# A decoder of six stages on one Trainium2 core: another hand-written order of the steps of its two attention stages, per engine

## What is computed

```python
x = ln(x + attention_with_conv_values(x))      # stage A
x = ln(x + cosine_cross(x, ctx))               # stage B
x = ln(x + gated_ternary_ffn(x))               # stage C
x = ln(x + relu_feature_attention(x))          # stage D: 16 heads of 16, 64 features, causal
x = ln(x + cross_attention(x, ctx))            # stage E: 16 heads of 16, softmax over 256 keys
x = ln(x + top2_of_8_experts(x))               # stage F
```

## Time and profile before

| | us |
|---|---|
| median of 3 runs (1478.37 to 1487.52) | 1481.47 |
| span of the profiled execution, first to last instruction | 1473.3 |
| TensorE busy | 1311.8 (89%) |
| VectorE busy | 911.7 (62%) |
| ScalarE busy | 573.1 (39%) |
| GpSimd busy | 795.9 (54%) |

### The profile page before, as it was taken

How to read it: one execution, slowest core, us unless ns; L and a number is a source line. 1 busy time by engine, 2 the same in 40 slices (tenths; PEclk the granted TensorE clock), 3 DMA queues, 4 the chain that set the end, 5 groups by cost and what they waited for, 6 DMA issues and landing times.

```text
span 1473.3 us, 23156 instructions
## 1 busy us (share of the span) xinstructions
PE 1311.8 (89%) x9073; PEld 1113.5 (76%) x9073; DVE 911.7 (62%) x1729; ACT 573.1 (39%) x1172; POOL 795.9 (54%) x761
## 2 busy tenths in 40 slices
PE   6998999999999999988899888987884699999980
PEld 6997788888888888866666666666653699999980
DVE  4656622632442262234687787777884699999966
ACT  3566311211121121124344444433342477777742
POOL 4444566666576576523232344535565347888831
PEclk9998999999999999999899999988885799999995
DMA  5101233233343233213324324235531755666605
GB/s 177 39 18 39 73 99 122 86 101 101 107 136 100 86 100 100 75 42 83 108 64 121 94 68 111 52 110 134 144 144 36 227 203 209 231 234 227 223 15 165
DMA packets 63101, 169.53 MB, mean 115 GB/s; under 512 B 11029, under 2 KB 30735, under 8 KB 55056
## 3 DMA queue, kind: packets, MB, share of 16 engines
q1 hardware_dynamic: 52432, 122.19, 27.8%
q0 software_dynamic: 10560, 45.86, 8.8%
HBM read 138.57 MB, written 33.38 MB: 117 GB/s over the span
## 4 chain that ended last, share of the span: by engine, by line
PE 71%; DVE 16%; ACT 3%; issue 3%; POOL 2%; DMA 2%; SPq 1%; ACTq 0%; POOLq 0%; DVEq 0%
PE bank L410 16%; PE bank L412 15%; PE bank L411 15%; PE bank L1297 9%; PE bank L418 4%; PE bank L1056 3%; PE bank L1137 3%; DVE topE L1809 3%; DVE shiftE L1816 3%; DVE topE L1811 1%; PE bank L1213 1%; ACT x_tok L458 1%; PE bank L1124 1%; PE bank L1192 1%; DVE x_tok L1977 1%
## 5 line engine op out<-in xcount | busy, mean ns | idle before, releaser
L1680 DVE CAST hid_hi<-bank 128x512 fp32r<-128x512 f32 x96 | 66.4, 691 | 252.1 <-ACT bank L1412 251.0
L552 POOL TENSOR_TENSOR wpiece_lo<-wraw,wpiece_hi 128x1024 fp32r<-128x1024 f32 x88 | 211.1, 2398 | 7.3
L410 PE MATMUL bank<-hid_hi,wpiece_lo 128*128 128x512 f32 x512 | 199.3, 389 | 0.0
L412 PE MATMUL bank<-hid_hi,wpiece_hi 128*128 128x512 f32 x512 | 199.2, 389 | 0.0
L411 PE MATMUL bank<-hid_lo,wpiece_hi 128*128 128x512 f32 x512 | 199.2, 389 | 0.0
L550 POOL TENSOR_SCALAR wpiece_hi<-wraw 128x1024 fp32r<-128x1024 f32 x88 | 94.1, 1069 | 154.7 <-PE bank L412 126.7
L1412 ACT ACTIVATE bank<-bank,ffn_scales 128x512 f32<-128x512 f32 x64 | 42.4, 662 | 301.5 <-PE bank L412 301.5
L1498 ACT ACTIVATE staging<-bank 128x512 f32<-128x512 f32 x128 | 70.0, 599 | 129.4 <-PE bank L1213 117.7
L412 PEld LDWEIGHTS bank<-hid_hi,wpiece_hi 128*128 128x128 f32 x512 | 96.1, 188 | 20.1
L410 PEld LDWEIGHTS bank<-hid_hi,wpiece_lo 128*128 128x128 f32 x512 | 96.1, 188 | 20.1
L411 PEld LDWEIGHTS bank<-hid_lo,wpiece_hi 128*128 128x128 f32 x512 | 96.1, 188 | 20.0
(11 more groups left out here) (342 smaller groups left out, 3696.9 us busy)
## 6 DMA issues: line engine op xcount, KB each, us to landing
wraw<-in_C_w SPq DMA_DIRECT2D x88, 512.0 KB, 3.6
w2raw<-in_F_w SPq DMA_DIRECT2D x8, 1152.0 KB, 7.2
w1raw<-in_F_w SPq DMA_DIRECT2D x8, 1028.0 KB, 7.4
split_qk<-qk_hi SPq DMA_DIRECT2D x64, 128.0 KB, 3.8
xt_lo<-split_qk SPq DMA_DIRECT2D x8, 1024.0 KB, 6.4
xt_hi<-split_qk SPq DMA_DIRECT2D x8, 1024.0 KB, 5.1
split_qk<-qk_lo SPq DMA_DIRECT2D x32, 128.0 KB
split_qk<-ctx_raw SPq DMA_DIRECT2D x32, 128.0 KB, 3.8
```

Of the source, the lines that this page charges most:

```text
L410: pe.e.matmul(o, sl, mh, start=start and i == 0, stop=False)
L412: made = pe.e.matmul(o, sh, mh, start=False, stop=stop and i == n - 1)
L552: pool.e.tensor_tensor(pair[1], raw, f(pair[0]), ALU.subtract).then_inc(done, 1)
```

## The change

`de_steps` now takes the engine, and makes one list for each. Two tables move steps: `LATER` shifts a step by rounds, `PLACE` gives it another priority; entries under "all" hold for every engine, "dve" and "pool" for one. The start of E is d + 19 for every sequence. Bank order follows PE's list; the sets of banks are as before.

```diff
-def de_steps():
+PLACE = {
+    "all": {("DPRE", 1): 0.5, ("EDR", 0, 0): 1.5, ("EFIN", 3): -1, ("EFIN", 5): 2.5, ("EPRE", 2): 1.5, ("EPRE", 3):
+            3.5, ("PAIR", 1): 0.5, ("PAIR", 2): -0.5, ("QUAD", 0): 4.5, ("QUAD", 2): -2, ("SLOTS", 0): -1, ("XT", 0):
+            0.5},
+    "dve": {("EFIN", 2): 3.5, ("EFIN", 6): 0.5, ("PAIR", 0): 0.5},
+    "pool": {("EFIN", 1): -0.5, ("EFIN", 6): -2},
+}
+LATER = {
+    "all": {("EDR", 0, 0): 1, ("EDR", 1, 0): -1, ("EFIN", 6): -1, ("EFIN", 7): 1, ("EPRE", 0): -1, ("EPRE", 1): -1,
+            ("EPRE", 3): 1, ("PAIR", 0): 1, ("QUAD", 2): -1, ("SLOTS", 0): 1, ("SLOTS", 2): -1, ("XT", 0): -1},
+}
+def de_items():
...
-        e = d + (20 if b < B - 2 else 22)
+        e = d + (19 if b < B - 2 else 19)
...
-    return in_rounds(items)
+    return items
+def de_steps(engine):
+    order = []
+    for n, (first, prio, name, args, at) in enumerate(de_items()):
+        for step, r in enumerate(range(at) if isinstance(at, int) else at):
+            q = prio if isinstance(prio, int) or isinstance(prio, float) else prio[step]
+            key = (name, args[1], step) if name in ("DDR", "EDR") else (name, step)
+            for who in ("all", engine):
+                r += LATER.get(who, {}).get(key, 0)
+                q = PLACE.get(who, {}).get(key, q)
+            order.append((first + r, q, first, n, name, step, args))
+    return [x[4:] for x in sorted(order)]
...
-AB, DE, FS, GS = ab_steps(), de_steps(), f_steps(), g_steps()
+AB, FS, GS = ab_steps(), f_steps(), g_steps()
+DE = {e: de_steps(e) for e in ("pe", "act", "dve", "pool", "sp")}
...
-            for name, step, args in DE:
+            for name, step, args in DE["pe"]:
```

More of the change, by code:

```diff
@@ L136, in g_steps @@
     return in_rounds([(b, 0, "SUM", (b,), 3) for b in range(B)])
-AB, DE, FS, GS = ab_steps(), de_steps(), f_steps(), g_steps()
+AB, FS, GS = ab_steps(), f_steps(), g_steps()
+DE = {e: de_steps(e) for e in ("pe", "act", "dve", "pool", "sp")}
 def bank_order():
-    every, low, held, upper, wide = range(8), range(6), range(6, 8), range(4, 8), range(8, 10)
+    every, low, held, upper = range(8), range(6), range(6, 8), range(4, 8)
+    wide_f, wide_s, wide_e = range(8, 10), range(8, 10), range(8, 10)
     out = []
@@ L168, in bank_order @@
         elif name == "QUAD" and step == 0:
-            out.append((("D", "f", *args), wide))
+            out.append((("D", "f", *args), wide_f))
         elif name == "QUAD" and step < 3:
-            out.append((("D", "s", *args, step - 1), wide))
+            out.append((("D", "s", *args, step - 1), wide_s))
         elif name == "QUAD":
@@ L178, in bank_order @@
         elif name == "PAIR" and step == 0:
-            out.append((("E", "s", *args), wide))
+            out.append((("E", "s", *args), wide_e))
         elif name == "PAIR" and step == 1:
@@ L640, in pool_program @@
                 pool.e.memset(v[:, :, :, DH:DH + 1], 1.0).then_inc(s_vone, 1)
-            for name, step, args in DE:
+            for name, step, args in DE["pool"]:
                 if name == "DPRE" and step == 0 and args[0] == 1:
@@ L861, in stack_heads @@
                      held.rearrange("i r (d j) s -> (i r d) (j s)", j=4), l_qk[b % 2])
-            for name, step, args in DE:
+            for name, step, args in DE["sp"]:
                 b = args[0]
@@ L1434, in finish @@
                     ln_apply(act, stage, b, resid[b % 2 if stage == "D" else 2])
-            for name, step, args in DE:
+            for name, step, args in DE["act"]:
                 if name == "CN":
@@ L1773, in finish @@
                     ln_scale(dve, stage, b)
-            for name, step, args in DE:
+            for name, step, args in DE["dve"]:
                 if name == "CN":
```

## The result

| | before | after |
|---|---|---|
| median, us | 1483.4 (1478.4 to 1487.5, 4 runs) | 1432.8 (1430.5 to 1433.7, 4 runs) |
| span of the profiled execution | 1473.3 | 1428.7 |
| mean granted clock of TensorE | 0.94 | 0.945 |

A forecast was written before the change was run, and what follows sets the result against it. TensorE was taken as nearly the bound, VectorE close behind, with waits for VectorE's shift deciding. Terms -5 - 13 - 8 = -26 gave a span of 1447.3 and, 8.2 above it, a median of 1455.5 us; range 1440 to 1476.

The forecast's parts named there:

- part 2: Attention stage: transposes and attention products one round closer to the scores; no wait added on TensorE, cost 0.
- part 1: Steady stretch: features late and D scores 1 first in the next odd round; -13 us.
- Part 1, the waits: Steady stretch: 10 of the 12.6 us that D scores wait for VectorE's shift taken as gone.
- Part 1, the clock: Steady stretch: fewer waits should leave fewer stretches at TensorE's lower clock; 3 us, ends 0 and 15.
- part 4: End of attention: sequences 6 and 7 start two rounds sooner; -8 us, ends 0 and -11.
- the 9.7 us: Steady stretch: E scores' waits for VectorE's shift, left unchanged; ends all gone or 11 us more.
- Part 3: Start of attention: keys a round sooner, context ahead of the norm; -5 us, ends -5.1 and +3.
- rival (c): End of attention: sequence 7 waits for its stack, so the end gains nothing; 1463.5 us, chance 0.10.
- Rival (a), the lock: Odd rounds: POOL's clamp blocks VectorE's through shared ports, losing 1.05 us each; slower, 1501.5 us, chance 0.07.
- Rival (b): Steady stretch: the same lock at half the time, part 1 comes to nothing; 1468.5 us, chance 0.18.
- Rival (d): Whole attention stage: everything idle goes, 30 + 5 + 11 = 46 us; 1435.5 us, chance 0.03.
- The signs: Right if D scores' shift waits under 4 us, context wait gone, sequence 6 within 7 us, sequence 2 in 52 to 53.

The follow-up runs named there:

- the pair steps back: Changed kernel with E's transposes again two rounds behind the scores, value product four and behind them, E's ending a round later: 1454.1 us, ratio 0.9832.
- the rungs: Kernel before with E's ending (and values product) a round sooner, 1471.2 us; value product also sooner and first, 1476.9 us; transposes also sooner, 1457.2 us.
- Taking the group back: Changed kernel with context, keys, queries and values of E back at their old rounds and priorities: 1452.3 us, ratio 0.982.
- the pair steps alone: Kernel before with E's transposes one round behind the scores, value product three behind and first, E's ending a round sooner: 1457.2 us, ratio 0.9852.

## Why the prediction was wrong, point by point

Two terms of the sum failed: part 2, put at nothing, which brings some 21 us when made alone, and the clock in part 1, put at 3 us. They lie in the steady part, which fell by 30.7 us (by 42 and 43 in the two profiles without the stall) where 13 were forecast.

- **What bounds the kernel**: right in the main. With 22 to 25 us of TensorE's waits for the shift the steady part took 311 to 319 us, with 2 to 11 us of them 268 to 305. Among these last they don't order the times: with the pair steps back there are 2.8 us of them and the part takes 297.3, with waits for ScalarE in their place.
- **Part 1, the waits**: 10 of 12.6 us were taken as gone; alone on the kernel before, the D scores' fell by 11.2 us, the E scores' by 3.5, and a wait that I hadn't named, features for the mask of D scores 1, came with 5.2. That sum (-9.5) is the forecast's -10, by luck in part: the new wait happens to cancel what the E scores gained.
- **Part 1, the clock**: mis-sized. "I take 3 us, ends 0 and 15": with this part alone TensorE's busy time fell by 9.8 us, with the whole change by 13.1 (and by 16.8 in a profile without the stall). By the estimate above, the clock's share is 9 of 13.1; without the stall the lower level falls from 32 to 3 us, which makes 14 of 16.8. The range was right, the pick wasn't; in sequence 2, where the clock was full before and after, the busy time fell by only 1.1 us (48.5 to 47.4).
- **Part 2, "Cost 0 here"**: the step that failed. It was argued that the transposes add no wait, which was so in the steady part (at the end it wasn't, see part 4), and taken that none goes, which wasn't so. Alone, these steps bring some 21 us: the waits for the shift fall from 22.3 to 9.1 us and TensorE's busy time by 7.8. E's ending goes one round sooner with them. That alone (with E's values product) takes the E scores' wait away and gives it to the D scores (24.8 us); the value product's round takes it from there and waits for POOL, and only the transposes' round is without either. Why it goes so is read from the waits; shown are the times of the rungs. "I leave the 9.7 us as they are" in part 1 is the same fault: in the whole change those waits fell to 2.7 us. On top of part 1 the steps bring less, 8 to 10 us (1456.5 to 1448.0, on two occasions).
- **Part 3**: direction right, size too small. The context's wait is gone, the stack's fell from 3.2 to 1.3 us, as worked out, but the first scores come 9.3 us sooner instead of 5. Of that, 1.2 us lie ahead of the first features; counted from these it is 8.1, and 6.4 and 6.9 in the two other profiles. Two more waits shrink that the sum hadn't (D scores for `feat`, 3.0 to 1.1 us, and 1.9 us in front of later features, for which the profile names no releaser). Taking the group back costs 7 us there, and 17 to 19 in the steady part and 8 before sequence 7, where the forecast had nothing for it.
- **Part 4**: first scores of 6 come 6.6 us after the last of 5, as said ("within 7"). From sequence 6 to 7 it takes 5.4 us more, without a wait for the stack worth naming (0.4 us), so rival (c) didn't happen; the end gained 5.6 of the 8 us. What has come there is a wait that part 2 had ruled out, of the transposes for the shift, 13.1 us behind 980.4 where it was 0.8 behind 1020.4:

```profile
PE bank L445 <- DVE shiftE L1843: 13.1, 9, 2.3
```

  There are no D scores there any more that would have waited for the shift first, and VectorE is busy for 32.3 of 36.9 and 22.2 of 24.8 us, as it was before; so whether this wait or VectorE's work holds back the rest of the 8 us isn't shown.
- **Around the span**: the forecast carried 8.2 us from the span of the profiled execution to the median; after, these are 4.1 us apart (1428.7 and 1432.8). So of the 22.7 us by which the median was missed, 18.6 lie in the span and 4.1 here. A run's time and its own span differ by only 1.8 us (1430.5 and 1428.7); what else lies between a span and the median is which execution was profiled, a quick one both times.
- **Rival (a), the lock**: the mechanism is there, the price isn't. Of 64 clamps on VectorE 25 took over 0.3 us more than the shortest, where it had been 15, yet the excess of all is the same (19.5 us, before 20.3), and mean 474 ns stands against 487. All of these 40 long clamps end within 0.05 us of the end of a POOL instruction, 23 of the 25 after beside POOL's clamp. The rule of the Trainium skill ("SBUF — State Buffer", "SBUF: two separate sides"), by which the one engine waits for the other's whole instruction, agrees with these long clamps; that it makes the round longer, as (a) had it, no run shows; TensorE's waits for the shift fell all the same.
- **Rival (b)**, half the time, rested on the 9.7 us where VectorE gets no relief; these went too.
- **Rival (d)**, all idle time goes (1435.5), was the closest, by luck: of its 30 us in the steady part 17.6 went and of its 11 at the end 5.6, and the busy time that went beside them it didn't name. Its argument against, VectorE over 86% busy, held nothing back: it is 86% busy in the steady part (240.4 of 280.3) and 90% in a profile without the stall (241.2 of 269.1).
- **The signs**: those of "right" came (no wait of the D scores for the shift, none for the context, 6.6 us to the first scores of 6), but sequence 2 took 49.4 us, not 52 to 53. So the mechanism of part 1 is there, and more beside it.

## What to carry to other kernels

Price a step that is moved for what it does to the rounds of the engine that others wait for, even if the step itself adds and removes no wait; a group of moves that buffers tie together can be worth 21 us where its first part alone is worth 6 and its first two together nothing. Don't judge by the largest wait in the table: the 84 us on ScalarE could be moved to other places without any gain, and 22 us in front of TensorE's scores were most of the idle time that there was to win. Where a lower clock stands in the row of a stretch with waits, give its rise a term of its own: here about 9 us beside 18 of idle time. And profile the same program more than once before you compare stretches: here one stall of 11 us was in one profile of it and not in two others.

## What was not expected of the hardware

Removing waits paid more than once: in the steady part TensorE lost 17.6 us of idle time and, for the same products, 13.1 us of busy time, of which about 9 go with the granted clock, 0.98 instead of 0.95. The clock doesn't follow the idle time alone, though. With the pair steps alone on the kernel before TensorE is idle for 19.6 us of the steady part and at the lower level for 9, with the pair steps taken back from the changed kernel it is idle for 21.4 us and at the lower level for 31. And one and the same program has, in some executions, a stall in which VectorE stands for 7 to 9 us, in the first profile TensorE and ScalarE with it; four copies beside it took 9.98 us instead of 2.4 there and their usual time in other profiles with it, and it comes with the scatters in their old places too.
